# Last layer of a four-layer kernel: who rounds and subtracts the projections, and where a unit's sums are copied

## The chip, the cores and the metric

The kernel runs on one core of one Trainium2 chip, as one program on five engines: TensorE (PE, with its weight loads PEld), VectorE (DVE), ScalarE (ACT), GpSimd (POOL) and SyncE (SP, which issues DMAs here). The metric is the device time of one execution in microseconds, the median of several.

## The reference, cut to what matters

Four layers work on `x` of 2 x 2048 tokens by 256 features, each as `x = x + attn(layernorm(x)) + ffn(layernorm(x))`. The change touches only the last one, whose attention is ordinary causal attention with 16 heads of 16 features:

```python
q = split_heads(einsum('bsd,kd->bsk', x, q_proj_weight))      # 16 heads of 16
k = split_heads(...); v = split_heads(...)
scores = einsum('bhtc,bhkc->bhtk', q, k) * 16 ** -0.5
attn = softmax(where(causal, scores, -inf), axis=-1)
out = einsum('bhtk,bhkc->bhtc', attn, v)                      # then the output projection
```

Its feed-forward part is `sqrt((x @ cos(a))**2 + (x @ sin(b))**2)`, called the phase below.

## The kernel before, in words

The attention of the last layer is cut into 32 units (j, n): j = 0 to 7 is one of two sequences and a group of four heads, n = 0 to 3 is a block of 512 queries. A unit goes through two stages.

*Prep.* `pe_qk` projects q and k of 512 tokens into one PSUM bank, name `qk` (two matmuls by the weights `aWqk`). The product q.k is to be nearly exact although TensorE rounds its inputs, so each projection is split into a rounded part and a rest. ScalarE copies the bank into `hi` with rounding (`act_qk`, L2885), then VectorE subtracts `hi` from the bank and writes `lo` (`dve_qk`, L2758), which also frees the bank. SyncE then copies rows of `hi` and `lo` into the operands `QS` and `KS` with 24 DMAs (`place`, L2459), so that one matmul over 48 rows adds the three partial products. Next, `pe_prep` forms score tiles of 128 queries by up to 512 keys (rows `ps<-KS,QS`), and VectorE takes the maximum of each (L2784, or L2787 where the tile crosses the diagonal). The maxima are transposed by `pe_max` (L2592), copied to `ms` by VectorE and written into row 48 of `QS` by SyncE (`shift`, L2468).

*Main.* For each block kt of 128 keys and each pair pr of heads, `pe_main` forms two transposed score tiles (rows `ps<-QS,KS`), ScalarE takes their exponentials into `P` (L2917), GpSimd clears what lies past the diagonal in the last four kt of a unit (L2974), and TensorE multiplies by `Va` (L2636, the PV product) into a bank of its own. One pass over kt and pr is called a step here; a unit has 8n + 8. At a unit's end ScalarE copies the sums of the PV bank to `osb` (L2931), TensorE spreads each head's denominator over its rows (the sum matmul `ps<-osb,selS`), ScalarE forms its reciprocal as exp(-ln) (L2900, L2903), GpSimd multiplies (`On`, L2964), TensorE projects twice (`ps<-On,aWo`) and VectorE adds to `xT` (L2814). What follows the copy is a generator, `finish`, of which one piece is run after each step of the next unit.

The work of all stages is merged into one order by `on_clock`: each stage has a time at which it begins and a pace, and whichever is earliest goes next. Every engine walks through this same merged order and issues only its own part. Main trails prep by five clock units; a j takes ten. Every score tile, projection, sum and output product takes the next bank of one ring of seven PSUM banks (`psx`), so a matmul waits until the content of seven fills earlier has been read by ScalarE or VectorE. `beside` puts the projection for two units ahead behind the first tile of a prep unit and the transposed maxima of the unit before behind the second. GpSimd has no part in prep; its main work is written out by hand in `pool_main`.

In steady state a j has four places where a projection lies in the main work: A, when prep of n = 0 starts (main is at kt 8 of n = 2); B, prep of n = 1, just behind the boundary between main n = 2 and 3; C, prep of n = 2, in the middle of main n = 3; D, prep of n = 3, just behind the boundary between main n = 0 and 1. Two further boundaries, E (n = 1 to 2) and F (n = 3 to 0), have no projection near them.

## Time and profile before

| | us |
|---|---|
| median of 3 runs | 3794.77 (3785.83 to 3804.28) |
| the profiled execution, span from first to last instruction | 3867.5 |
| TensorE busy in it | 3519.2 (91%) |
| VectorE busy | 2473.4 (64%) |
| ScalarE busy | 1730.0 (45%) |
| GpSimd busy | 1164.8 (30%) |

Only the span is known of the profiled execution: what lies around it is not recorded apart, and with the profiler on it is longer than any of the three timed runs. A busy engine in the profile is one that has an instruction in flight. Matmul ends are modelled, so a matmul that stands in a group with a wait inside it still counts as busy. The last layer's attention takes the stretch from about 2730 us to the end.

### The profile page before, as it was taken

To read this page: it belongs to the slowest core of one execution; us is meant where nothing else is said; L and a number is where in the kernel's file an instruction comes from. 1 tells how busy PE (TensorE), PEld (TensorE's weight loads), DVE (VectorE), ACT (ScalarE), POOL (GpSimd) and SP (SyncE) were. 2 spreads that over 40 slices of the span, in tenths; PEclk is the share of its full clock that TensorE was granted. 3 is DMA by queue.
4 is the path that set the end of the run, shared out by engine and by line. 5 is a ranking of instruction groups with operands and counts; after the bars stand their busy time and mean duration, and the time that the engine had idled before them with its cause. 6 is when DMAs were issued, how large, how long until landed. Compare 5 with 4: busy or idle time off the path is not lost.

```text
span 3867.5 us, 47778 instructions
## 1 busy us (share of the span) xinstructions
PE 3519.2 (91%) x16468; PEld 2089.1 (54%) x16468; DVE 2473.4 (64%) x6381; ACT 1730.0 (45%) x3237; POOL 1164.8 (30%) x1190
## 2 busy tenths in 40 slices
PE   8899999968898988989878999998899999999998
PEld 7677777734555545545546667676543333433332
DVE  4444443455788988889865443443568788678774
ACT  2234443322234423343344544443346666666667
POOL 0322222151355555555542322223211111011111
PEclk7799999988899999999989999999889899999999
DMA  3244445321466666666750000000101011111100
GB/s 109 73 165 168 177 180 180 128 66 71 136 204 193 216 211 194 197 204 197 212 187 3 0 1 1 1 1 9 38 20 31 20 23 34 31 34 27 32 18 23
DMA packets 107154, 368.87 MB, mean 95 GB/s; under 512 B 27248, under 2 KB 41088, under 8 KB 96928
## 3 DMA queue, kind: packets, MB, share of 16 engines
q0 software_dynamic: 57664, 302.82, 24.3%
q1 hardware_dynamic: 48160, 60.90, 5.6%
q8 instruction: 131, 2.15, 0.2%
q10 hardware_dynamic: 1088, 2.10, 0.2%
q14 instruction: 111, 0.91, 0.1%
HBM read 322.59 MB, written 17.69 MB: 88 GB/s over the span
## 4 chain that ended last, share of the span: by engine, by line
PE 66%; DVE 21%; ACT 6%; issue 4%; another core or an unknown queue 2%; POOL 1%; DMA 0%; POOLq 0%; DVEq 0%; SPq 0%; ACTq 0%
PE ps L184 51%; PE ps L2636 6%; DVE pm L2784 4%; PE ps L1507 2%; DVE mi L1642 2%; DVE gathB L1719 2%; DVE ps L2787 2%; DVE hacc L1682 2%; ACT P L2917 1%; PE ps L2126 1%; DVE mx L1638 1%; PE ps L556 1%; PE ps L581 1%; PE ps L546 1%
## 5 line engine op out<-in xcount | busy, mean ns | idle before, releaser
L2917 ACT ACTIVATE P<-ps 128x512 f32<-128x512 f32 (+3 forms) x1280 | 587.3, 548 | 214.1 <-PE ps L184 212.0
L2784 DVE TENSOR_REDUCE pm<-ps 128x1 f32<-128x512 f32 x768 | 484.6, 684 | 113.3 <-PE ps L184 113.0
L1860 POOL DMA_INDIRECT gathB<-in_tab,idx x256 | 282.9, 1105 | 357.6 <-PE ps L1507 287.4
L184 PE MATMUL ps<-QS,KS 49*128 49x512 f32 (+3 forms) x1280 | 333.8, 422 | 16.2 <-DVE pm L2784 12.6
L1860 POOL DMA_INDIRECT gathA<-in_tab,idx x256 | 268.7, 1049 | 203.2 <-DVE mx L1638 125.5
L184 PE MATMUL ps<-KS,QS 48*128 48x512 f32 (+3 forms) x1280 | 309.8, 430 | 16.0 <-DVE pm L2787 5.9
L2974 POOL TENSOR_SCALAR_AFFINE_SELECT P<-P 128x256 f32<-128x256 f32 x256 | 103.8, 409 | 709.9 <-ACT P L2917 709.0
L2636 PE MATMUL ps<-P,Va 128*32 128x512 f32 (+3 forms) x2560 | 309.7, 557 | 5.8 <-POOL P L2974 2.9
L184 PEld LDWEIGHTS ps<-QS,KS 49*128 49x128 f32 x1280 | 158.2, 190 | 225.0 <-DVE pm L2784 81.8
L184 PEld LDWEIGHTS ps<-KS,QS 48*128 48x128 f32 x1280 | 145.5, 191 | 212.8 <-DVE pm L2784 66.2
L2787 DVE CUSTOM_DVE_ANT_0 ps<-ps,past 128x128 f32<-128x128 f32 (+3 forms) x512 | 240.1, 515 | 26.6 <-PE ps L184 24.6
L184 PE MATMUL ps<-f,K 128*128 128x512 f32 x1024 | 249.3, 395 | 0.0
L184 PE MATMUL ps<-WS,xn 128*128 128x512 f32 x512 | 231.4, 593 | 0.0
L184 PEld LDWEIGHTS ps<-f,K 128*128 128x128 f32 x1024 | 192.2, 188 | 46.8
L184 PE MATMUL ps<-moe,FW 128*128 128x128 f32 x1704 | 205.1, 278 | 0.3 <-ACT moe L1164 0.3
L184 PEld LDWEIGHTS ps<-moe,FW 128*128 128x128 f32 x1704 | 199.2, 195 | 0.5 <-ACT moe L1164 0.5
L1194 POOL DMA_INDIRECT FW<-in_F,fidx x71 | 71.6, 1009 | 414.0 <-PE ps L184 252.0
L1719 DVE CUSTOM_DVE_ANT_0 gathB<-hg,gathB,gte 128x512 f32<-128x512 f32 x256 | 178.3, 750 | 0.9 <-DMA gathB<-in_tab,idx 0.9
L1682 DVE SCALAR_TENSOR_TENSOR hacc<-gathA,lin,hacc 128x512 f32<-128x512 f32 x224 | 168.6, 753 | 3.9 <-DVE hacc L1682 0.5
L2387 POOL TENSOR_TENSOR f<-fa,f 128x512 fp32r<-128x512 f32 x64 | 85.5, 1336 | 258.4 <-DVE f L2259 258.4
L184 PEld LDWEIGHTS ps<-WS,xn 128*128 128x128 f32 x512 | 95.8, 191 | 111.5 <-issue 107.0
L998 DVE TENSOR_TENSOR moe<-moe,ps 128x384 f32<-128x384 f32 x71 | 39.4, 555 | 180.8 <-PE ps L184 121.5
(390 smaller groups left out, 7002.8 us busy)
## 6 DMA issues: line engine op xcount, KB each, us to landing
ys_sorted<-moe SPq DMA_DIRECT2D x71, 128.0 KB
KS<-hi SPq DMA_DIRECT2D x256, 32.0 KB, 1.9
QS<-hi SPq DMA_DIRECT2D x256, 32.0 KB, 1.9
gathA<-in_tab,idx POOLq DMA_INDIRECT x256
gathB<-in_tab,idx POOLq DMA_INDIRECT x256
KS<-lo SPq DMA_DIRECT2D x128, 32.0 KB, 1.9
QS<-lo SPq DMA_DIRECT2D x128, 32.0 KB, 2.0
out<-xT SPq DMA_DIRECT2D x8, 512.0 KB, 3.2
```

Of the source, the lines that this page charges most:

```text
L184: m = pe.matmul(out, w, x, start=start and i == 0, stop=stop and i == len(pairs) - 1, skip_group_check=True)
L1507: pe.matmul(p[:, ms], GB[:, h, 512 + m * 128:640 + m * 128], dg[h], start=False, stop=h == 7, skip_group_check=True).then_inc(*PR.pe.tick( ...
L1642: v = dve.max_index(mi[:, 4 * g + i, :], mx[:, 4 * g + i, :], p[:, i * 128:(i + 1) * 128])
L1682: dve.scalar_tensor_tensor(out=hacc[:, :], in0=GA[:, h, 256:768], scalar=lin[:, h:h + 1], in1=src, op0=ALU.mult, op1=ALU.add).then_inc(*(P ...
L1719: dve.tensor_tensor_reduce(out=GB[:, h, 0:512], in0=hg[:, :], in1=GB[:, h, 0:512], scale=gt_[:, h:h + 1], scalar=0.0, op0=ALU.mult, op1=AL ...
L1860: pool.indirect_dma_start(out=(GA, GB)[half][:, h, :], out_offset=None, in_=d[f"tab{half}"], in_offset=bass.IndirectOffsetOnAxis(ap=idx[t ...
L2387: pool.tensor_tensor(f2[m % 2][:, 1, :], fa[:, (m + 2) % 3, :], f2[m % 2][:, 0, :].bitcast(F32), ALU.subtract).then_inc(*BN.pool.tick("f2" ...
L2636: m = pe.matmul(o_[32 * hd:32 * hd + 32, off:BW], Va[:, kt, h * 17:h * 17 + 32], Pb[2 * (kt % 2) + hd // 2][:, hd % 2, off:BW], start=kt = ...
L2784: v = dve.tensor_reduce(m, p, AX.X, ALU.max)
L2787: v = dve.tensor_tensor_reduce(out=p, in0=p, in1=past[:, 512 - w:512], scale=1.0, scalar=-3.0e38, op0=ALU.add, op1=ALU.max, accum_out=m)
L2917: act.activation(P_[:, hh, off:BW], psx.tile("s2", j, n, kt, pr, hh)[:, off:BW], ACT.Exp).then_inc(*psx.emptied(MN.act, "s2", j, n, kt, pr ...
L2974: pool.affine_select(out=P_, in_=P_, compare_op=ALU.is_ge, fill=0.0, base=0, pattern=[[0, 2], [1, 128]], channel_multiplier=-1).then_inc(* ...
```

## The change

Five things are done, all in the last layer.

1. `act_qk` copies the projection twice: with rounding to `hi`, and without to `lo`. The second copy frees the bank.
2. `dve_qk` is gone. A new `pool_qk` on GpSimd subtracts `hi` from `lo` in SBUF, at the merged order's next place ("max" instead of "qk"), and `place` waits for it.
3. The copy of the PV sums to `osb` moves from the end of a unit into `finish`, behind the exponentials of the next unit's first step. ScalarE's logarithm comes two steps later than before, and its exponential of it as well.
4. TensorE's sum matmul, its two output products and VectorE's additions come one step later; GpSimd's `On` is tied to the fifth step.
5. GpSimd now walks through the merged order as well. Its memset of `Va`, which stood ahead of all its phase additions, now lies near their end.

```diff
--- before.py
+++ after.py
@@ -2449,7 +2449,7 @@
                     bs = slice(n * BW, (n + 1) * BW)
                     sp.wait_ge(*WT.pool.has(f"KS{j % 2}"))
                     sp.wait_ge(*MN.pe.has("s2", j - 2, 3, 4 * n + 3, 1, 1))
-                    sp.wait_ge(*PP.dve.has("qk", j, n))
+                    sp.wait_ge(*PP.pool.has("qk", j, n))
                     for col, to, places in ((1, KS, ((hi, 0), (hi, 16), (lo, 32))), (0, QS, ((hi, 0), (lo, 16), (hi, 32)))):
                         for pr in range(2):
                             for hh in range(2):
@@ -2639,6 +2639,7 @@
                     m.then_inc(*MN.pe.tick("pv", j, n, kt))
 
                 def finish(n):
+                    yield
                     p = psx.fill("sum", j, n)
                     pe.wait_ge(*MN.act.has("o", j, n))
                     pe.wait_all(psx.freed("sum", j, n))
@@ -2751,12 +2752,6 @@
                         dve.tensor_tensor(blk(xT, m, n), blk(xT, m, n), tmp[2 * ((2 * n + m) % 3)], ALU.add).then_inc(
                             *x_add(None, n, "phase", n, m))
                         yield
-
-            def dve_qk(dve, j, n):
-                dve.wait_ge(*placed_before(j, n))
-                dve.wait_ge(*PP.act.has("hi", j, n))
-                dve.tensor_tensor(lo[at(j, n)][:, :], psx.tile("qk", j, n), hi[at(j, n)][:, :].bitcast(F32), ALU.subtract).then_inc(
-                    *psx.emptied(PP.dve, "qk", j, n))
 
             def dve_maxima(dve, j, n, pr):
                 dve.wait_ge(*PP.dve.now())
@@ -2792,8 +2787,6 @@
                             yield
                             step += 1
                             also = beside(n, step)
-                            if also == "qk" and ahead(j, n)[0] < NJ:
-                                dve_qk(dve, *ahead(j, n))
                             if also == "max" and preceding(j, n)[0] >= 0:
                                 dve_max(dve, *preceding(j, n))
                             if also:
@@ -2806,7 +2799,7 @@
             def dve_main(dve, j, n, tail, v):
                 def finish(n):
                     b = j // 4
-                    yield from nothing(5)
+                    yield from nothing(6)
                     for m in range(2):
                         dve.wait_ge(*MN.pe.has("out", j, n, m))
                         dve.wait_ge(*x_before(4 * b + n))
@@ -2839,7 +2832,7 @@
                     yield from dve_weights(dve)
                     yield from dve_phase(dve)
 
-                dve_all(dve, everything(lambda j, n: dve_qk(dve, j, n), phase, lambda j, n: dve_prep(dve, j, n), lambda: nothing(8),
+                dve_all(dve, everything(lambda j, n: None, phase, lambda j, n: dve_prep(dve, j, n), lambda: nothing(8),
                                     lambda j, n: dve_main(dve, j, n, tail, nothing(8) if (j, n) == (3, 3) else iter(())), lambda: dve_last(dve)))
                 tail.drain()
 
@@ -2882,7 +2875,9 @@
             def act_qk(act, j, n):
                 act.wait_ge(*placed_before(j, n))
                 act.wait_ge(*PP.pe.has("qk", j, n))
-                act.activation(hi[at(j, n)][:, :], psx.tile("qk", j, n), ACT.Copy).then_inc(*PP.act.tick("hi", j, n))
+                act.activation(hi[at(j, n)][:, :], psx.tile("qk", j, n), ACT.Copy)
+                act.activation(lo[at(j, n)][:, :].bitcast(F32), psx.tile("qk", j, n), ACT.Copy).then_inc(
+                    *psx.emptied(PP.act, "qk", j, n))
 
             def act_prep(act, j, n):
                 for step in range(1, 8 * n + 9):
@@ -2896,6 +2891,9 @@
             def act_main(act, j, n, tail, v):
                 def finish(n):
                     act.wait_ge(*MN.pool.has("on", *((j, n - 1) if n else (j - 1, 3))))
+                    act.wait_ge(*MN.pe.has("pv", j, n, 4 * n + 3))
+                    act.activation(osb[:, :], po.tile("o", j, n)[:, :], ACT.Copy).then_inc(*po.emptied(MN.act, "o", j, n))
+                    yield from nothing(2)
                     act.wait_ge(*MN.pe.has("sum", j, n))
                     act.activation(inv[:, :], psx.tile("sum", j, n), ACT.Ln).then_inc(*psx.emptied(MN.act, "sum", j, n))
                     yield
@@ -2925,10 +2923,7 @@
                 yield
                 for _ in v:
                     pass
-                act.wait_ge(*MN.pool.has("on", *((j, n - 1) if n else (j - 1, 3))))
-                act.wait_ge(*MN.pe.has("pv", j, n, 4 * n + 3))
                 tail.drain()
-                act.activation(osb[:, :], po.tile("o", j, n)[:, :], ACT.Copy).then_inc(*po.emptied(MN.act, "o", j, n))
                 tail.gen = finish(n)
                 yield
 
@@ -2954,29 +2949,49 @@
                         pool.tensor_tensor(s0, s0, s1, ALU.add).then_inc(*PH.pool.tick("sum", n, m))
                         yield from nothing(3)
 
-            def pool_main(pool, j):
-
-                def divide(j, n):
-                    if j < 0:
-                        return
+            def pool_qk(pool, j, n):
+                pool.wait_ge(*PP.act.has("qk", j, n))
+                pool.tensor_tensor(lo[at(j, n)][:, :], lo[at(j, n)][:, :].bitcast(F32), hi[at(j, n)][:, :].bitcast(F32),
+                                   ALU.subtract).then_inc(*PP.pool.tick("qk", j, n))
+
+            def pool_prep(pool, j, n):
+                for step in range(1, 8 * n + 9):
+                    yield
+                    also = beside(n, step)
+                    if also == "max" and ahead(j, n)[0] < NJ:
+                        pool_qk(pool, *ahead(j, n))
+                    if also:
+                        yield
+
+            def pool_main(pool, j, n, tail, v):
+
+                def finish(n):
+                    yield from nothing(4)
                     pool.wait_ge(*MN.pe.has("out", *preceding(j, n), 1))
                     pool.wait_ge(*MN.act.has("inv", j, n))
                     pool.tensor_tensor(On[:, :], osb[:, :], inv[:, :], ALU.mult).then_inc(*MN.pool.tick("on", j, n))
-
-                for n in range(NQ):
-                    if n:
-                        divide(*preceding(j, n))
-                    for kt in range(4 * n, 4 * n + 4):
-                        off = (kt - 4 * n) * 128
-                        for pr in range(2):
+                    yield
+
+                for kt in range(4 * n + 4):
+                    off = (kt - 4 * n) * 128
+                    for pr in range(2):
+                        if kt >= 4 * n:
                             P_ = Pb[2 * (kt % 2) + pr][:, :, off:off + 128]
                             pool.wait_ge(*MN.act.has("s2", j, n, kt, pr, 1))
                             pool.affine_select(out=P_, in_=P_, compare_op=ALU.is_ge, fill=0.0, base=0, pattern=[[0, 2], [1, 128]],
                                                channel_multiplier=-1).then_inc(*MN.pool.tick("causal", j, n, kt, pr))
-                        if kt == 0:
-                            divide(*preceding(j, n))
-                if j == NJ - 1:
-                    divide(j, NQ - 1)
+                        yield
+                        tail.step()
+                        if pr == 1 and kt:
+                            if kt % 2 and kt > 2:
+                                next(v, None)
+                            yield
+                yield
+                for _ in v:
+                    pass
+                tail.drain()
+                tail.gen = finish(n)
+                yield
 
             def pool(pool):
                 pool.memset(past[:, :], 0.0).then_inc(*WT.pool.tick("past0"))
@@ -2986,13 +3001,23 @@
                 for i in range(2):
                     pool.memset(QS[i][:, :, :].bitcast(F32), 0.0)
                     pool.memset(KS[i][:, :, :].bitcast(F32), 1.0).then_inc(*WT.pool.tick(f"KS{i}"))
-                pool.wait_ge(*WT.act.total())
-                pool.wait_ge(*LN.pe.total())
-                pool.memset(Va[:, :, :], 1.0).then_inc(*PP.pool.tick("Va1"))
-                for _ in pool_phase(pool):
+                tail = Tail()
+
+                def ones():
+                    pool.wait_ge(*WT.act.total())
+                    pool.wait_ge(*LN.pe.total())
+                    pool.memset(Va[:, :, :], 1.0).then_inc(*PP.pool.tick("Va1"))
+                    yield from nothing(8)
+
+                def phase():
+                    yield from nothing(TURN)
+                    yield from pool_phase(pool)
+
+                for _ in everything(lambda j, n: pool_qk(pool, j, n), phase, lambda j, n: pool_prep(pool, j, n), ones,
+                                    lambda j, n: pool_main(pool, j, n, tail, nothing(8) if (j, n) == (3, 3) else iter(())),
+                                    lambda: nothing(1)):
                     pass
-                for j in range(NJ):
-                    pool_main(pool, j)
+                tail.drain()
 
             return {"pe": pe, "dve": dve, "act": act, "pool": pool, "sp": sp}
```

On TensorE at place D (the boundary from main unit (2, 0) to (2, 1)), in the kernel before, from the last PV product of the old unit on; `QS0,KS0` rows are main's score tiles, `KS0,QS0` rows prep's, `xn3,aWqk` is the projection:

```order
L2636 MATMUL ps3<-P3,Va 32x128 x2
L184 MATMUL ps1<-QS0,KS0 128x512 x2
L184 MATMUL ps2<-KS0,QS0 128x512 x2
L184 MATMUL ps3<-osb,selS 128x512
L184 MATMUL ps0<-QS0,KS0 128x512 x2
L184 MATMUL ps1<-xn3,aWqk 128x512 x2
L184 MATMUL ps1<-QS0,KS0 128x512
L184 MATMUL ps2<-QS0,KS0 128x512
```

The same place in the changed kernel:

```order
L2636 MATMUL ps3<-P3,Va 32x128 x2
L184 MATMUL ps1<-QS0,KS0 128x512 x2
L184 MATMUL ps2<-KS0,QS0 128x512 x2
L184 MATMUL ps3<-QS0,KS0 128x512
L184 MATMUL ps0<-QS0,KS0 128x512
L184 MATMUL ps0<-xn3,aWqk 128x512 x2
L184 MATMUL ps1<-osb,selS 128x512
L184 MATMUL ps1<-QS0,KS0 128x512
L184 MATMUL ps2<-QS0,KS0 128x512
```

The sum matmul has moved behind the score tiles of the second step and behind the projection.

On ScalarE at the same place, before, from the copy of the sums on (`P` rows are the exponentials):

```order
L2931 ACTIVATE osb<-ps3 128x512
L2917 ACTIVATE P0<-ps1 128x512 x2
L2900 ACTIVATE inv<-ps3 128x512
L2917 ACTIVATE P1<-ps0 128x512 x2
L2885 ACTIVATE hi1<-ps1 128x512
L2903 ACTIVATE inv<-inv 128x512
L2917 ACTIVATE P2<-ps1 128x512
L2917 ACTIVATE P2<-ps2 128x512
L2917 ACTIVATE P3<-ps0 128x512 x2
```

And in the changed kernel, from the first exponentials of the new unit on:

```order
L2915 ACTIVATE P0<-ps1 128x512 x2
L2895 ACTIVATE osb<-ps3 128x512
L2915 ACTIVATE P1<-ps3 128x512
L2915 ACTIVATE P1<-ps0 128x512
L2878 ACTIVATE hi1<-ps0 128x512
L2879 ACTIVATE lo1<-ps0 128x512
L2915 ACTIVATE P2<-ps1 128x512
L2915 ACTIVATE P2<-ps2 128x512
L2898 ACTIVATE inv<-ps1 128x512
L2915 ACTIVATE P3<-ps0 128x512 x2
L2901 ACTIVATE inv<-inv 128x512
```

The copy stands one pair of exponentials later, the second projection copy is new, and the two instructions on `inv` have moved from around the projection to behind it.

On GpSimd around place A in the changed kernel (the diagonal block of main unit (2, 2), between the product `On` of the unit before and of this one):

```order
L2972 TENSOR_TENSOR On<-osb,inv 128x512
L2981 AFFINE_SELECT P0<-P0 128x2x128
L2981 AFFINE_SELECT P1<-P1 128x2x128
L2981 AFFINE_SELECT P2<-P2 128x2x128
L2981 AFFINE_SELECT P3<-P3 128x2x128
L2954 TENSOR_TENSOR lo2<-lo2,hi2 128x512
L2981 AFFINE_SELECT P0<-P0 128x2x128
L2981 AFFINE_SELECT P1<-P1 128x2x128
L2981 AFFINE_SELECT P2<-P2 128x2x128
L2981 AFFINE_SELECT P3<-P3 128x2x128
L2954 TENSOR_TENSOR lo0<-lo0,hi0 128x512
```

Before, the eight selects stood in a row here. Now a subtraction lies between the fourth and the fifth.

## Rows read from the trace of the kernel before

**Rows 1.** The page's first part, busy time of the engines.

```profile
PE 3519.2 (91%) x16468; PEld 2089.1 (54%) x16468; DVE 2473.4 (64%) x6381; ACT 1730.0 (45%) x3237; POOL 1164.8 (30%) x1190
```

**Rows 2.** Windows: one j; length, busy of five engines, PEclk, DMA share, GB/s.

```profile
3141.44:3262.04 120.60, 114.89 (x686) 45.51 (x688) 98.65 (x248) 81.39 (x177) 18.04 (x36) 1.00 0.13 28
```

**Rows 3.** The chain that ended last between 2870 and 3750 us, by line.

```profile
by line: PE ps L184 43.8%; PE ps L2636 22.1%; DVE pm L2784 17.1%; DVE ps L2787 6.9%; ACT P L2917 3.7%; issue 1.7%; ACT hi L2885 1.0%; DVE pm L2787 0.9%; ACT inv L2903 0.6%; DVE lo L2758 0.6%; ACT osb L2931 0.5%; DVE mz L2764 0.4%; ACT inv L
```

**Rows 4.** Groups from 2600 us on: busy, mean ns, then idle before and releaser.

```profile
L2758 DVE TENSOR_TENSOR lo<-ps,hi 128x512 fp32r<-128x512 f32 x32 | 22.1, 692 | 72.9 <-ACT hi L2885 72.9
L2885 ACT ACTIVATE hi<-ps 128x512 fp32r<-128x512 f32 x32 | 19.1, 597 | 49.1 <-PE ps L184 49.1
L2931 ACT ACTIVATE osb<-ps 128x512 f32<-128x512 f32 x32 | 19.2, 599 | 52.2 <-PE ps L2636 52.2
L2964 POOL TENSOR_TENSOR On<-osb,inv 128x512 f32<-128x512 f32 x32 | 40.9, 1279 | 160.5 <-ACT inv L2903 134.4 <-PE ps L184 26.2
```

**Rows 5.** Waits in the same j as Rows 2: us in total, times, longest.

```profile
PEld ps L184 <- DVE pm L2784: 18.7, 33, 0.8
PEld ps L184 <- ACT P L2917: 13.9, 29, 0.8
ACT osb L2931 <- PE ps L2636: 6.3, 4, 1.9
```

**Rows 6.** Timeline at place C: start, us, instruction, count [idle before <-releaser].

```profile
3224.57 1.98 PE L184 MATMUL ps<-xn,aWqk 128*128 128x512 f32 x4
3226.65 0.60 ACT L2885 ACTIVATE hi<-ps 128x512 fp32r<-128x512 f32 x1 [2.09 <-PE ps L184]
3227.06 0.40 PE L184 MATMUL ps<-KS,QS 48*128 48x512 f32 x2
3227.15 4.03 ACT L2917 ACTIVATE P<-ps 128x512 f32<-128x512 f32 x8
3227.35 0.69 DVE L2758 TENSOR_TENSOR lo<-ps,hi 128x512 fp32r<-128x512 f32 x1 [1.86 <-ACT hi L2885]
...
3228.42 1.34 PE L184 MATMUL ps<-QS,KS 49*128 49x512 f32 x4
...
3229.26 0.18 PEld L184 LDWEIGHTS ps<-QS,KS 49*128 49x128 f32 x1 [0.31 <-ACT P L2917]
...
3231.28 2.49 DVE L2784 TENSOR_REDUCE pm<-ps 128x1 f32<-128x512 f32 x4 [0.84 <-PE ps L184]
```

**Rows 7.** Timeline at place D, same columns.

```profile
3142.45 4.01 ACT L2917 ACTIVATE P<-ps 128x512 f32<-128x512 f32 x8
3142.70 1.28 POOL L2964 TENSOR_TENSOR On<-osb,inv 128x512 f32<-128x512 f32 x1 [6.65 <-ACT inv L2903]
3142.75 1.28 DVE L2784 TENSOR_REDUCE pm<-ps 128x1 f32<-128x512 f32 x2
...
3147.74 1.09 ACT L2917 ACTIVATE P<-ps 128x512 f32<-128x512 f32 x2 [1.28 <-PE ps L184]
...
3149.30 1.07 PE L2636 MATMUL ps<-P,Va 128*32 128x512 f32 x8
```

**Rows 8.** Timeline at place A, same columns.

```profile
3192.01 0.18 PEld L184 LDWEIGHTS ps<-KS,QS 48*128 48x128 f32 x1 [0.20 <-ACT P L2917]
...
3192.03 0.41 POOL L2974 TENSOR_SCALAR_AFFINE_SELECT P<-P 128x256 f32<-128x256 f32 x1 [0.36 <-ACT P L2917]
...
3192.59 0.60 DVE L2787 CUSTOM_DVE_ANT_0 ps<-ps,past 128x384 f32<-128x384 f32 x1
```

**Rows 9.** Timeline at place B, same columns.

```profile
3207.77 1.09 ACT L2917 ACTIVATE P<-ps 128x512 f32<-128x512 f32 x2 [1.78 <-PE ps L184]
```

**Rows 10.** Timeline at the layer's start, and SyncE's issues at place A.

```profile
2776.21 3.94 POOL L2991 MEMSET Va<- 128x4608 f32 x1 [57.23 <-PE ps L184]
2790.59 0.30 PEld L184 LDWEIGHTS ps<-xn,P 128*128 128x128 f32 x2 [0.47 <-DVE pm L2787]
...
3194.84 1.55 SPq L2459 DMA_DIRECT2D KS<-hi  x2
```

## The prediction

> **What bounds the kernel now.** I began with the busy shares of the page [rows 1]. TensorE has 91% over the whole kernel and everything else far less, so work taken from another engine is worth only what TensorE waited for it. The change touches the last layer alone, so next came the windows of one j of its attention [rows 2]. At the full clock a j takes 120.60 us. TensorE shows 114.89 of these, VectorE 98.65, ScalarE 81.39, GpSimd 18.04. The reader should see that nobody is saturated except, by this count, TensorE, and that VectorE is the second. But a matmul row that contains a wait still counts as busy, so the third view was the chain of waits [rows 3]: TensorE holds about 66% of it, VectorE's maxima (L2784, L2787) 25%, the exponentials 3.7%. The steps that the change edits are small in it: `hi` 1.0%, `lo` 0.6%, `osb` 0.5%. Over the 880 us of that view these are 8.8, 5.3 and 4.4 us. That is the most that the three can give back if their place on the chain vanishes and nothing takes it.
>
> The waits of that j show the coupling [rows 5]. TensorE's weight loads wait 18.7 us for the maxima and 13.9 us for the exponentials; parts of both lie under a PV product that is still running. Score tiles for both readers share one ring of seven banks, so TensorE is held by whichever reader is late at that moment, ScalarE or VectorE. What must be asked at each projection is therefore: who frees the bank that TensorE wants next?
>
> **The change part by part.** I replay places of one j with the durations of its rows. All sums are in the time of the profiled execution, whose span of 3867.5 us is 72.7 us (1.9%) above the median; I carry the difference over to the median unscaled.
>
> *VectorE loses the subtraction.* It is 32 instructions of 692 ns, 22.1 us in all, and before them VectorE stood idle for 72.9 us waiting for `hi` [rows 4]. This looks like 95 us of relief. Most of it is not. During the projection TensorE makes no score tile for 1.98 us, so VectorE would idle there anyway. At C [rows 6] the next tiles for VectorE are started at 3227.06, take 0.40, and so are ready at about 3227.5; the subtraction occupies VectorE from 3227.35 for 0.69, to 3228.0. The real relief is some 0.5 us there. For the other places I take the length of the subtraction itself, 0.7, as the bound. Four places in each of seven j at 0.7 give 20 us, reached only if VectorE is what TensorE waits for right behind every projection.
>
> *ScalarE gains a copy.* A copy takes 597 ns [rows 4] and costs the row of instructions behind it 0.50 us, as eight exponentials in a row take 4.03 us [rows 6]. There are 32, 16 to 19 us of ScalarE's time. ScalarE has 39 us of idle time in a j [rows 2], but not at this spot: at C it has just waited 2.09 us for the projection, eight exponentials are due behind `hi`, and TensorE already needs 1.34 us for four score tiles because weight loads wait for exponentials (0.31 at 3229.26) [rows 6]. Every exponential there comes 0.50 later, so do the tiles, the PV product behind them and the next tiles for VectorE, which stands idle for them by 0.84 before 3231.28. Nobody downstream is ahead, so the shift stays: +0.5 us. At A the same holds by one bank: the second of two prep tiles waits at 3192.01 for an exponential and is read at about 3192.59 [rows 8]. Started at 3192.01 it is ready after the 0.40 of such a pair plus some 0.1, at 3192.5; with the copy that becomes 3193.0, and VectorE starts 0.4 late: +0.4 us. The relief ahead of it is lost in that wait.
>
> *The copy of the sums and what follows it.* Before, ScalarE stood idle 6.3 us per j, at four boundaries, for the last PV product [rows 5], then copied for 0.60 [rows 4], while TensorE made the next unit's first tiles in about 0.40 [rows 6]. Behind the change the wait is for those tiles, so ScalarE's idle time stays and the first exponentials come only 0.2 us earlier. At B and D, however, the logarithm used to lie ahead of the projection, in time when ScalarE had nothing to do; it now lies behind it, together with the second copy. From `hi` to the end of eight exponentials ScalarE has two instructions more, 1.0 us by 0.50 each. Against this the projection starts a little earlier, because the sum matmul stands behind it. At D the eight exponentials ended at 3146.46 and the next pair began at 3147.74, after 1.28 us of idle time [rows 7]; at B that idle time is 1.78 us [rows 9]. These gaps absorb a delay of 0.5 to 1.0 us. What is left at D is that the first output product now wants a bank of the last of these exponentials; my replay brings the PV product of 3149.30 [rows 7] to 3149.45: +0.15 us. At B I get 0. At E and F I find nothing beyond 0.3 of either sign and take 0. Bounds for a boundary: -0.2 (the earlier exponentials, fully used) to +1.0 (both instructions, nothing absorbed).
>
> *GpSimd subtracts.* The trace has no such instruction; the nearest is `On`, the same form over two SBUF tiles, 1279 ns [rows 4]. 32 of them are 41 us on an engine busy for 18 of 120 us. The rest is ready about 1.2 us later than before (0.5 for the copy, 1.28 against 0.69 for the subtraction). Who waits for it is SyncE's `place`: at A its first DMA goes out at 3194.84 [rows 10], behind the shift. The subtraction there stands behind the select that ran at 3192.03 for 0.41 [rows 8]; with the exponentials 0.5 later it runs from 3192.9 to 3194.2, still in time. The placed rows themselves are wanted two prep units later. I cost it at nothing; uncovered it would be 1.2 us per place. It also stands ahead of four selects at A, at most 1.28 us on a PV product; I take 0, since tiles and exponentials are late there by 0.4 to 0.5 anyway, and keep the 1.28 for the third rival.
>
> Whether the pass disturbs VectorE can be read: an `On` ran from 3142.70 while VectorE did two maxima in 1.28 us [rows 7], and four of them elsewhere take 2.49 [rows 6], so the maxima don't slow. The Trainium skill, "SBUF — State Buffer", section "Who interferes with whom", says that the two engines share a port pair as an exclusive lock, but that a VectorE instruction takes it only in a two-port mode or with both inputs in SBUF, and that a reduction never contends. Here each of VectorE's steady instructions reads PSUM; by that rule, the trace agrees, and nothing is added. Without its exception the rule would add up to 32 x 1.28 = 41 us.
>
> *The start.* The memset of `Va`, 3.94 us, stood ahead of the first phase addition at 2776.21 [rows 10]. It now lies between the last two of sixteen additions, where GpSimd has little to do, and ahead of the first copy to `Va`; there it could hold ScalarE by at most its 3.94 us. TensorE did not stand still for it: its visible wait in that stretch is 0.47 us at 2790.59 [rows 10]. So -0.5 us, bounds -3.94 and +3.94.
>
> **The sum.** Each place is met seven times with both stages running: 7 x (0.4 at A + 0 at B + 0.5 at C + 0.15 at D) = 7.4, less 0.5 at the start: +7 us. On the median that is 3794.8 + 7 = 3802 us, +0.2%. A difference of under 0.5% (19 us) can hardly be told from no change in measurements of this kernel.
>
> **The rivals.**
> 1. *VectorE's relief is worth its full size.* For it: the maxima are 25% of the chain and make TensorE wait more often than the exponentials do. Against it: right behind the projections the waits shown are for exponentials. If at every place TensorE is held by VectorE, the gain is 28 x 0.7 = 20 us, plus 0.2 at 31 boundaries, 26 us: 3769 to 3775.
> 2. *ScalarE becomes the bound around projections and boundaries.* Each of 28 places costs the full 0.50 (14 us), and at 14 of them (B, D) the delayed logarithm and its exponential cost up to 0.50 each more because the gaps of 1.28 and 1.78 us are not used, as TensorE needs a bank inside them: 14 us. Together +28: 3823. It decides as soon as the idle time behind B and D is gone for TensorE's purposes.
> 3. *GpSimd's order delays selects, `On`, or VectorE.* `On` follows the logarithm by fewer steps than before, and at F it has to let five selects pass and stands ahead of three. If output products wait 1.28 us at 28 places, that is +36: 3831. For it is only how tight the order is; against it is that GpSimd is busy for 15% of the time.
> 4. *No effect at all:* VectorE's relief and ScalarE's load cancel at each place: 3795. I count it with the forecast.
>
> **How the numbers follow.** Forecast with its neighbour 4: 0.58, own range 3788 to 3812. Rival 1: 0.20. Rival 2: 0.16. Rival 3: 0.06. For the range I reach half-way into rival 1 and to rival 2's value: 3777 to 3823. Rival 1 gives most of faster (0.19); part of 2 and all of 3 give slower (0.21); the rest is same (0.60).
>
> **What would show it.** In the changed profile a j at full clock should take 121 to 122 us, VectorE's busy time in it fall by 2.8 us and ScalarE's rise by about 2. Behind `hi` at A and C, weight loads should wait longer for exponentials (L2915) and less for maxima. The idle time behind the eight exponentials at B and D should shrink from 1.78 and 1.28 to about 1. `place` should still begin behind the shift. I am wrong if the waits for exponentials do not grow behind projections, if the j gets shorter than 120 us, or if output products are seen to wait for `On`.

## The result, and the profile after

The changed kernel takes 3842.14 us (median of four runs, 3839.38 to 3844.98) against 3794.47 us for the kernel before on the same chip: a ratio of 1.012, 95% interval 1.0101 to 1.014. The forecast of 3802 us and its range up to 3823 us were wrong; the change costs about 48 us by the medians.

The page of the changed kernel, busy time of the engines (answers to [rows 1]), and below it its groups of instructions from 2600 us on (answers to [rows 4]; L2954 is the subtraction, L2879 the second copy):

```profile
PE 3529.5 (92%) x16468; PEld 2087.1 (54%) x16468; DVE 2452.2 (64%) x6349; ACT 1740.2 (45%) x3269; POOL 1207.4 (31%) x1222
```

```profile
L2954 POOL TENSOR_TENSOR lo<-lo,hi 128x512 fp32r<-128x512 f32 x32 | 41.0, 1282 | 262.5 <-ACT lo L2879 262.5
L2972 POOL TENSOR_TENSOR On<-osb,inv 128x512 f32<-128x512 f32 x32 | 40.8, 1276 | 128.2 <-ACT inv L2901 65.3 <-PE ps L184 62.8
L2895 ACT ACTIVATE osb<-ps 128x512 f32<-128x512 f32 x32 | 19.3, 603 | 1.1 <-PE ps L2636 1.1
L2878 ACT ACTIVATE hi<-ps 128x512 fp32r<-128x512 f32 x32 | 19.1, 596 | 47.7 <-PE ps L184 47.7
L2879 ACT ACTIVATE lo<-ps 128x512 f32<-128x512 f32 x32 | 18.9, 591 | 0.0
```

Single instructions cost what was forecast: a copy 0.59 us, the subtraction on GpSimd 1282 ns where 1279 was taken from `On`, and ScalarE's wait for the last PV product is gone (1.1 us in all). What they do to TensorE shows in windows. Their columns are those of [rows 2]. First the kernel before: all attention from the fifth `hi` to the end, then the four stretches of the j of [rows 2] from one `hi` to the next, that is D to A, A to B, B to C and C to D. The column before the last two is the granted clock; a value between 0.50 and 1.00 is a mix of TensorE's two levels, 1.2 and 2.4 GHz.

```profile
2840.42:3867.50 1027.08, 970.38 (x5537) 387.87 (x5535) 763.15 (x1895) 662.78 (x1441) 145.66 (x289) 0.96 0.11 27
...
3141.44:3189.83 48.39, 46.42 (x273) 17.91 (x275) 39.94 (x90) 33.44 (x70) 6.65 (x12) 1.00 0.08 17
3189.83:3200.96 11.13, 10.69 (x73) 4.76 (x75) 9.22 (x34) 7.29 (x19) 2.40 (x6) 1.00 0.12 25
3200.96:3226.65 25.69, 24.76 (x139) 9.20 (x141) 19.94 (x54) 17.54 (x34) 1.27 (x1) 1.00 0.20 45
3226.65:3262.04 35.39, 33.02 (x207) 13.64 (x209) 29.56 (x70) 23.13 (x55) 7.72 (x17) 1.00 0.13 30
```

The same of the changed kernel:

```profile
2773.18:3843.20 1070.02, 1004.52 (x5537) 404.19 (x5535) 749.41 (x1867) 672.20 (x1469) 183.64 (x318) 0.92 0.11 26
...
3074.73:3124.49 49.76, 47.62 (x275) 18.29 (x275) 39.56 (x89) 34.29 (x71) 7.92 (x13) 1.00 0.08 17
3124.49:3137.66 13.17, 12.84 (x70) 6.07 (x71) 8.86 (x33) 7.17 (x19) 3.55 (x7) 0.74 0.13 29
3137.66:3164.37 26.71, 25.25 (x141) 9.30 (x141) 19.24 (x53) 18.61 (x36) 2.56 (x2) 1.00 0.21 47
3164.37:3203.27 38.90, 36.22 (x204) 14.68 (x205) 29.18 (x69) 22.92 (x54) 9.00 (x18) 0.87 0.10 21
```

Two things are to be read. First, stretches at the full clock are longer: 49.76 for 48.39 and 26.71 for 25.69 us; A to B is 11.18 where it is undisturbed. (The sum matmul, 1.0 us, moves from ahead of `hi` to behind it at B and D, so single stretches shift; only the sum over a j counts.) Second, the granted clock of the attention is 0.92 instead of 0.96. Windows of 2 us give the time at the lower level, 1.2 GHz, as 166 us instead of 86. A profile of a second run of the changed kernel (run 10) shows 131 us.

Only the last layer is compared here, since the profiled execution of before had its own 1.9% extra elsewhere. From its first `hi` to the end it takes 1138.0 us before and 1176.9 after, 38.9 more. Against the 48 us of the medians that leaves 9 which this pair of profiles does not show.

### The profile page after: what moved, and what is told of

Its sections match the earlier page's. It is cut to its first block, busy times and chain, and to the rows that moved or that the text cites. A ratio compares the mean times of both kernels' runs of the same rounds, so it can differ in the third digit from the quotient of the medians.

```text
span 3843.2 us, 47788 instructions
## 1 busy us (share of the span) xinstructions
PE 3529.5 (92%) x16468; PEld 2087.1 (54%) x16468; DVE 2452.2 (64%) x6349; ACT 1740.2 (45%) x3269; POOL 1207.4 (31%) x1222
## 4 chain that ended last, share of the span: by engine, by line
PE 67%; DVE 23%; ACT 6%; issue 3%; POOL 1%; DMA 0%; DVEq 0%; POOLq 0%; SPq 0%; ACTq 0%
PE ps L184 52%; PE ps L2636 6%; DVE pm L2779 4%; DVE mi L1642 3%; PE ps L1507 2%; DVE hacc L1682 2%; DVE gathB L1719 2%; DVE ps L2782 2%; ACT P L2915 2%; PE ps L2126 1%; DVE mx L1638 1%; PE ps L556 1%; DVE tm L1596 1%; PE ps L546 1%; PE ps L581 1%
## 5 line engine op out<-in xcount | busy, mean ns | idle before, releaser
L2636 PE MATMUL ps<-P,Va 128*32 128x512 f32 (+3 forms) x2560 | 318.0, 571 | 4.9 <-POOL P L2981 2.9
L998 DVE TENSOR_TENSOR moe<-moe,ps 128x384 f32<-128x384 f32 x71 | 39.3, 554 | 179.3 <-PE ps L184 121.6
```

Of the source, the lines that this page charges most:

```text
L2636: m = pe.matmul(o_[32 * hd:32 * hd + 32, off:BW], Va[:, kt, h * 17:h * 17 + 32], Pb[2 * (kt % 2) + hd // 2][:, hd % 2, off:BW], start=kt = ...
```

## The experiments

Four theories were kept apart: **C**, each copy of ScalarE behind a projection is paid by TensorE; **S**, the later sum matmul and chain cost at the boundaries; **R**, the two instructions of the inverse lie in ScalarE's way; **K**, the clock falls more often. Ratios are to before on the same chip in the same session. In the table, "clean j" is the sum of the four stretches at the full clock (before: 120.60), "low" the attention's time at 1.2 GHz in the profile (before: 86 us). "Split" is the change's second copy and GpSimd's subtraction, "finish" the later copy of the sums and everything behind it; all versions but the seventh keep GpSimd's new order. The numbers of "clean j" are those of a j in which the four stretches could be read at the full clock, or are put together from several j; for the changed kernel C to D is an estimate, since none of its profiles has one at the full clock. A range says that they differ from j to j; before itself has later j of up to 121.4.

| run | what | ratio, 95% interval | clean j | low |
|---|---|---|---|---|
| 1 | split alone | 1.0041, 1.0020 to 1.0061 | 122.55 | 100 |
| 2, 14 | finish alone | 1.0071, 1.0049 to 1.0093; 1.0079, 1.0047 to 1.0111 | 122.4 | 100, 111 |
| 3 | whole change, logarithm a step earlier | 1.0101, 1.0048 to 1.0155 | 122.9 | 175 |
| 4, 15 | GpSimd's order alone | 0.9978, 0.9957 to 0.9999; 0.9985, 0.9957 to 1.0013 | 120.6 | 88, 70 |
| 5 | finish, sum matmul in the third step | 1.0074, 1.0041 to 1.0107 | some 121.5 | 133 |
| 6 | finish, inverse of 8 columns | 1.0021, 0.9985 to 1.0057 | 120.9 | 79 |
| 7 | before, inverse of 8 columns | 0.9969, 0.9936 to 1.0001 | 119.9 | 55 |
| 8 | split with a third copy | 1.0111, 1.0079 to 1.0142 | 124.54 | 112 |
| 9 | whole change, spare product in step 1 | 1.0103, 1.0067 to 1.0139 | 124 | 123 |
| 10 | whole change again | 1.0116, 1.0085 to 1.0148 | 123.4 | 131 |
| 11 | finish, but sums copied at the unit's end | 1.0078, 1.0051 to 1.0106 | 122.48 | 107 |
| 12 | sums copied late, sum matmul in step 1 | 1.0304, 1.0260 to 1.0348 | none | 272 |
| 13 | finish, spare product in step 1 | 1.0022, 0.9994 to 1.0050 | 122.5 to 123.2 | 62 |
| 16 | whole change, spare products in step 1 and in the last pair of steps | 1.0075, 1.0049 to 1.0100 | 126.5 to 128 | 10 |
| 17 | order alone, spare product in the last pair of steps | 1.0022, 1.0005 to 1.0039 | 123.4 to 123.8 | 24 |
| 18 | order alone, spare product in step 2 | 1.0002, 0.9983 to 1.0021 | 121.6 to 123 | 31 |

**The halves (runs 1, 2, 4).** Run 1 leaves `finish` as before; run 2 leaves `hi` and `lo` as before; run 4 has only `pool_main` rewritten and the memset of `Va` moved.

> Only the first half of the change: ScalarE's two copies, GpSimd's subtraction in the merged order; the sums are copied at the unit's end as before. Theory S (sum's bank): the loss comes from the other half, where the sum matmul's bank is freed two steps later, by the logarithm, and the transposed maxima seven fills behind it wait for that. Then this kernel takes before plus the 0.4 to 0.5 us of the extra copy at places A and C, less up to 4 us at the start: 3790 to 3802 us. Theory C (copy): the extra copy on ScalarE is the loss; then 3825 us or more. Theory K (clock): the loss is TensorE time at half clock; then the time follows the half-clock time in the last layer, whichever half of the change is in: more than 86 us of it with a slower kernel.

> Only the second half: the sums are copied behind the next unit's first exponentials, everything of finish one step later; VectorE still subtracts. Theory S: this half carries most of the loss, 3815 to 3840 us, and TensorE's transposed maxima (L2592) wait for the logarithm at places B and D. Theory C: 3790 to 3800 us.

> The kernel before, with nothing changed but GpSimd's walk through the merged order: the memset of Va near the end of the phase additions, the output product right behind the second step. The changed kernel reached its fifth projection 4 us sooner after the first than the kernel before. If the memset's place is why, this kernel is 3 to 4 us faster than before: 3791 us. If it is not (the clock or the missing subtraction), 3794 us.

> The version with GpSimd's new order and the memset of Va between the phase additions, nothing else changed. If its 4 us at the start are all that it brings: ratio 0.998 to 1.0, and a clean j of 120.6.

The split half costs 0.41% and the finish half 0.71%; their sum, 1.12%, is the whole within the intervals. On the 3794.5 us of before, run 1's 0.41% makes 3810 us, which lies between what its two theories forecast (3802 at most, 3825 at least). The order alone costs nothing. It does not hold the subtraction nor the later `On`, so for the third rival the waits of the changed kernel decide: over the last layer TensorE's weight loads wait 4.9 us for `On` (4.2 before) and 14.8 us for selects (14.7 before). That rival is out. One j of run 1, stretch by stretch:

```profile
3066.81:3115.68 48.87, 46.54 (x273) 18.02 (x275) 39.48 (x89) 33.90 (x70) 7.87 (x13) 1.00 0.08 17
3115.68:3127.29 11.61, 11.17 (x73) 4.92 (x75) 8.79 (x33) 7.76 (x20) 3.56 (x7) 1.00 0.11 25
3127.29:3153.51 26.22, 24.86 (x139) 9.20 (x141) 19.40 (x53) 18.01 (x36) 2.51 (x2) 1.00 0.21 46
3153.51:3189.36 35.85, 33.48 (x207) 13.81 (x209) 28.95 (x69) 23.59 (x55) 8.99 (x18) 1.00 0.12 27
```

Against before that is +0.48, +0.48, +0.53 and +0.46. A stretch holds the copy of the projection at its start, so these are D, A, B and C: the copy is paid in full behind all four projections, with VectorE's 2 us of relief in the same rows (98.65 to 96.62). TensorE's weight loads wait 17.1 us for exponentials in this j (13.9 before) and 18.4 for the full-width maxima (18.7). Run 8 doubles the suspected cost:

```diff
+                act.activation(spare[:, :], psx.tile("qk", j, n), ACT.Copy)
```

> e1 with a third copy of each projection, into a spare tile that nobody reads. Theory C (each ScalarE instruction behind a projection is paid in full at every place): each of the four intervals of a j grows by another 0.50 us, 122.55 to 124.5 us, and the time by 14 us over e1's 3816.5: 3830. If ScalarE's idle time behind B and D can absorb copies, as the prediction had it, only the two intervals behind A and C grow: 3823.

Each stretch grew by another 0.5 us (49.33, 12.11, 26.71 and 36.35 at the full clock). C stands for the split alone.

**Where the finish half loses (runs 3, 5, 6, 7, 11, 12).** Its clean j is 1.8 us longer; in some of the later j it is less, since D there costs nothing. Run 3 takes one empty step away from ScalarE ahead of the logarithm, run 5 puts one ahead of the sum matmul, runs 6 and 7 compute the inverse for 8 of the 512 columns in all units but the first.

```diff
-                    yield from nothing(2)
+                    yield from nothing(1)
```

> The changed kernel with the logarithm (and its exponential) one step earlier, so that the bank of the sum matmul is freed one step earlier. Theory S: the waits of L2592 and of the tiles behind it for the logarithm go, 10 to 20 us less than the changed kernel: 3820 to 3832 us. Theory C: no difference from the changed kernel, 3842 us within 5.

> The second half of the change alone (e2), with the sum matmul one step later still, in the third step instead of the second. It then finds the copy osb done, and its bank is no longer the one that the transposed maxima take. Theory S (TensorE's waits for the copy and for the logarithm are the loss of this half): at full clock prep n=1 to prep n=2 falls from 26.7 us to 26.2 or less, a j from 122.3 to 121.5 or less, and the time by 5 to 15 us below e2's 3824.6. Theory R (the logarithm and its exponential simply lie in ScalarE's row behind the projection, whoever waits for the bank): no change of the intervals by over 0.3 us, 3824 us within 5.

```diff
-                    act.activation(inv[:, :], psx.tile("sum", j, n), ACT.Ln)
+                    act.activation(inv[:, 0:w_], psx.tile("sum", j, n)[:, 0:w_], ACT.Ln)
```

> e2 with the logarithm and its exponential over 8 of 512 columns (behind the first unit; the rest of the reciprocals is left stale, so the result is not the reference's). Theory R: each of the two takes about 0.4 us out of ScalarE's row behind a projection, so prep n=1 to n=2 falls by 0.5 to 0.8 us to about 25.9 to 26.2, and a j by 1.5 us or more, more than in the kernel before with the same cut. Theory S: at most the 0.25 us of the bank goes.

> The kernel before with the same cut as e6 (logarithm and exponential over 8 columns, result left stale). In it the logarithm lies in time when ScalarE waits for TensorE anyway, so a j shortens by the exponential at places B and D at most: 120.6 to 119.6 us or more; time 3790 to 3801 us.

An earlier logarithm gave back 0.25 us (B to C, 26.46). With a short inverse the finish half still costs 1.0 us of a j (120.9 against 119.9), so R is at most the other 0.8. Run 5, with the sum matmul later still, gives back some 0.9 us (B to C 26.04), but at a lower clock (0.937 beside 0.944 for before), and its ratio is no better; the 5 to 15 us that theory S had forecast did not come. Run 11 then puts the copy of the sums back at the unit's end and leaves only the chain late; run 12 moves the copy and leaves the sum matmul in its step (the logarithm comes one step later there, the output products and additions one, and `On` three, so it is not the copy alone).

> The kernel before, its output sums still copied at the unit's end, with only the chain behind it one to two steps later: sum product in the second step, logarithm in the third, and so on to the output products. Theory S (the loss at the boundaries, 1.84 us per j in the version with the finish half alone, comes from the sum product's and the chain's later place): same loss, a clean j of 122.0-122.6, ratio 1.006 to 1.008. Theory O (it comes from the copy's place behind the first exponentials): a clean j within 0.5 us of 120.6, ratio 0.999 to 1.002.

> The kernel before with the copy of the output sums moved behind the next unit's first two exponentials, and everything else left in its step: sum product still in the first step (TensorE then waits for the copy there), logarithm in the second. Theory O: the copy's place costs by itself, 0.4-0.6 us at each boundary and more at the sum product, a clean j of 122.4 or more, ratio 1.007 or more. Theory S: the sum product keeps its filling place but waits about 0.5-0.7 us for the copy, so a clean j of 121 to 122, and falls of the clock at E and F stay as rare as before.

Run 11, the four stretches:

```profile
2984.77:3034.56 49.79, 47.86 (x275) 18.38 (x275) 40.27 (x90) 33.78 (x70) 6.62 (x12) 1.00 0.08 17
3034.56:3045.26 10.70, 10.08 (x70) 4.76 (x71) 9.21 (x34) 6.69 (x19) 2.39 (x6) 1.00 0.11 25
3045.26:3071.98 26.72, 25.49 (x141) 9.37 (x141) 19.86 (x54) 18.12 (x35) 1.28 (x1) 1.00 0.21 46
3071.98:3107.25 35.27, 32.85 (x204) 13.60 (x205) 29.55 (x70) 22.31 (x54) 7.65 (x17) 1.00 0.12 27
```

These are run 2's stretches (49.50 to 49.8, 10.70, 26.71, 35.24) to a few hundredths. Once the sum matmul comes a step later, where ScalarE copies the sums does not matter; the later sum matmul and chain are the whole loss of this half. Run 12 shows the reverse: with the sum matmul in step 1 TensorE stands still for the late copy, and the clock falls often (272 us at 1.2 GHz). Theory O had put the ratio at 1.007 or more, theory S a j at 121 to 122 us with falls at E and F as rare as before; both reckoned with delays of 0.4 to 0.7 us at a boundary, and neither with a loss of 3%. Its timeline at E, where TensorE waits 1.55 us:

```profile
2875.51 0.60 ACT L2900 ACTIVATE osb<-ps 128x512 f32<-128x512 f32 x1
...
2876.17 0.50 PEld L184 LDWEIGHTS ps<-osb,selS 128*128 128x128 f32 x2 [1.86 <-ACT osb L2900]
2876.17 2.07 PE L184 MATMUL ps<-osb,selS 128*128 128x512 f32 x2 [1.55 <-ACT osb L2900]
```

Why the place matters can be seen in the timelines of E. Before, at full clock:

```profile
3160.77 0.49 PE L184 MATMUL ps<-QS,KS 49*128 49x512 f32 x2
...
3161.11 0.58 PE L184 MATMUL ps<-KS,QS 48*128 48x512 f32 x2
...
3161.88 1.10 PE L184 MATMUL ps<-osb,selS 128*128 128x512 f32 x2 [0.19 <-DVE pm L2784]
...
3162.91 0.57 PE L184 MATMUL ps<-QS,KS 49*128 49x512 f32 x2
```

After:

```profile
3096.12 0.18 PEld L184 LDWEIGHTS ps<-QS,KS 49*128 49x128 f32 x1 [0.41 <-DVE pm L2779]
3096.12 1.09 PE L184 MATMUL ps<-QS,KS 49*128 49x512 f32 x2
3096.67 0.60 ACT L2895 ACTIVATE osb<-ps 128x512 f32<-128x512 f32 x1
3096.72 0.18 PEld L184 LDWEIGHTS ps<-QS,KS 49*128 49x128 f32 x1 [0.41 <-DVE pm L2779]
3097.32 0.19 PEld L184 LDWEIGHTS ps<-KS,QS 48*128 48x128 f32 x2 [0.41 <-DVE pm L2779]
...
3097.74 1.12 PE L184 MATMUL ps<-osb,selS 128*128 128x512 f32 x2
```

At this boundary VectorE is behind: before, it does six maxima in a row from 3159.25 on (3.68 us) without idle time. That it is behind because main's last tiles were narrow and came fast is my reading, not shown by a run. Before, the sum matmul, 1.1 us of dense work that needs one bank, filled the time in which VectorE freed the next. Now TensorE walks through three waits of 0.41 us for VectorE, one tile at a time, and does the 1.1 us afterwards.

Two of the runs below bear this out. Run 13 puts a spare product of the same size where the sum matmul had been, four more per j. Stretch for stretch its j is only about 0.3 us longer than run 2's (from C on 35.69, 49.49, 10.89 and 26.71, for 35.54, 49.50, 10.70 and 26.71): the place takes such a product almost for nothing. Run 18 puts it into the second step, behind a sum matmul that kept the first, and there four of them make a j 0.8 to 1.6 us longer than the same j of run 4.

**The clock (runs 9, 10, 13, 14, 16 to 18).** In the versions with the finish half the clock falls at another place than before: 0.7 to 3.9 us behind the copy of the sums at E and F (10 of the 17 falls in run 10's profile; before has none at E and two at F, 6 to 7 us behind). E is the clear mark: at F, run 4, without the finish half, has three falls 0.8 to 3.0 us behind the copy too, but neither it nor runs 1 and 15 has one at E. The changed kernel at one such E, windows of 2 us from 2 us ahead of the copy:

```profile
2837.24:2839.24 2.00, 1.79 (x14) 0.84 (x6) 2.00 (x4) 0.97 (x2) 0.00 (x0) 1.00 0.24 52
2839.24:2841.24 2.00, 1.83 (x4) 0.69 (x4) 1.97 (x7) 1.58 (x4) 0.00 (x0) 0.66 0.13 30
2841.24:2843.24 2.00, 2.00 (x4) 0.49 (x6) 1.07 (x2) 0.00 (x0) 0.00 (x0) 0.50 0.00 0
2843.24:2845.24 2.00, 2.00 (x10) 0.81 (x14) 0.96 (x2) 1.39 (x3) 0.00 (x0) 0.50 0.00 0
```

The second window, in which it falls, holds four matmul records. The sum matmul behind it takes 2.06 us instead of 1.12, and ScalarE stands idle for 3.03. So a spare product was put back where the sum matmul had been, into the bank that is really filled next, with a result that nobody reads:

```diff
                 def finish(n):
+                    i_ = psx.i % len(psx.tiles)
+                    pe.wait_all([s_.has(*k_) for s_, k_ in psx.empty.get(psx.last[i_], [])])
+                    chain(pe, psx.tiles[i_][:, :], [(WQK[:, 0, 0, :], xn[:, 0, 0:BW])])
                     yield
```

> The changed kernel, with one spare product put back where the sum product stood before: in the first step of each unit TensorE multiplies projection weights by 512 columns of xn into the bank that it will really fill next (its result is overwritten; TensorE's work grows by one product per unit, no engine waits for it). Theory K2 (the changed kernel leaves TensorE a thin stretch of waiting and short tiles at the boundaries, because the dense sum product has gone from there, and its clock then falls): falls right behind the copy of the output sums at boundaries E and F vanish, the half-clock time in the attention drops from 166 us to 100 or less, the mean clock is back within 0.002 of before's, and the ratio comes down from 1.012 to 1.005-1.009, though TensorE does more. Theory W (the falls come with any delay, wherever it lies): falls unchanged, the product costs up to 0.5 us at 28 boundaries, ratio 1.012 to 1.016.

> The changed kernel itself once more, as the neighbour of the one with the spare product on the same chip. All theories: ratio 1.010 to 1.014. Theory K2 also expects the falls of the clock again at E and F, right behind the copy of the output sums, and 130 to 190 us of half clock in the attention; a theory that the first profile was an outlier expects under 100.

> The version with the finish half alone (VectorE still subtracts, ScalarE copies a projection once) with the spare product in the first step of each unit. Theory K2: no falls behind the copy of the output sums at E and F, none new at B and D since ScalarE has no second copy there, half-clock time in the attention 60 to 95 us instead of the unfilled version's, mean clock higher than the unfilled one's by 0.002 or more, and a lower time than the unfilled one by 3 us or more although TensorE multiplies more. Theory W (the falls come with any lost time, wherever it lies): they appear elsewhere, the mean clock stays, and the time is equal to or above the unfilled one's.

> The version with the finish half alone once more, as the neighbour of the one with the spare product. Both theories: ratio 1.005 to 1.009, falls of the clock at E and F right behind the copy of the output sums.

On the finish half alone the outcome is plain: TensorE does 64 more matmul records, none of the falls 0.7 to 3.9 us behind the copy of the sums at E and F is left, the mean clock of eleven runs is 0.9426 beside 0.9353 for its unfilled neighbour, run 14 (before on that chip: 0.9390), and the ratio drops from 1.0079 (1.0047 to 1.0111) to 1.0022 (0.9994 to 1.0050). The two intervals touch; set against each other directly, the eleven runs of each have means of 3871.5 and 3884.8 us, 0.3% apart with an interval of 0.1 to 0.6%. The same boundary in run 13, the two windows from the copy on:

```profile
2904.26:2906.26 2.00, 1.68 (x6) 0.73 (x6) 1.97 (x7) 1.69 (x4) 0.00 (x0) 1.00 0.15 33
2906.26:2908.26 2.00, 2.00 (x12) 0.71 (x15) 1.48 (x3) 0.64 (x2) 0.00 (x0) 1.00 0.00 0
```

On the whole change (run 9) the falls at E and F were gone as well, but four came 16 to 17 us behind C instead, in the narrow last tiles just ahead of F, where before and run 10 have one each. The mean clock rose from 0.9358 (run 10, on the same chip) to 0.9406, of 0.9451 for before, and the ratio did not move measurably: 1.0103 beside 1.0116. The theory that the thin stretch at E and F is the cause had forecast more, 1.005 to 1.009 and at most 100 us at 1.2 GHz where 123 were measured, so for the whole change one spare product is not enough. Run 16 adds a second spare product there (`if kt == 4 * n + 3 and pr == 0`).

> The changed kernel with a spare product in the first step of each unit and a second one in each unit's last pair of steps, where the tiles are 128 columns wide and TensorE waits for maxima. Theory K2 (falls follow stretches in which TensorE has short tiles and waits): the falls 16 to 17 us behind D vanish too, mean clock at or above before's, ratio 1.003 to 1.008. Theory W (falls come with lost time, wherever it lies): the falls move again and the added work is paid, ratio 1.010 to 1.016.

(What it calls 16 to 17 us behind D is the place behind C, by the places of the prediction.)

Its attention, and one j of it:

```profile
2771.32:3819.30 1047.98, 994.43 (x5665) 395.61 (x5663) 751.86 (x1867) 673.89 (x1469) 183.48 (x318) 0.99 0.11 26
...
2943.48:3069.98 126.50, 121.63 (x701) 47.28 (x700) 97.16 (x244) 83.19 (x180) 22.98 (x40) 1.00 0.12 26
```

Two falls are left, the second 1.2 us ahead of the end, of 17 in run 10's profile; the mean clock of its runs is 0.956 beside 0.947 for before. A j at full clock is 3 us longer than the unfilled one's, and yet the ratio is 1.0075 (1.0049 to 1.0100) instead of 1.012 (1.0101 to 1.0140). That speaks against the theory that falls come with lost time wherever it lies. Runs 17 and 18 put the same product into the version with the order alone:

> The version with GpSimd's new order alone (0.998 of before), with a spare product in each unit's last pair of steps. Theory K2: mean clock above before's by 0.002 or more, which is worth 5 us or more, against at most 0.3 us paid at each of 28 places (8 us): ratio 0.995 to 1.001. Theory W: clock as before, ratio 1.000 to 1.003.

> The same version with the spare product in the second step of each unit instead, behind the sum product, which keeps the first. The mirror of the finish half with a spare product in the first step. If the chain's later steps cost nothing and the later product does: the ratio of that version, 1.001 to 1.004. If the spare product hides in TensorE's wait for maxima and only the chain's later steps cost: 0.996 to 1.000, with a mean clock above before's.

The clock rose here too (0.9535 and 0.9508 beside 0.9472), but not by more than the added work costs: about 3 us of a clean j in run 17, where at most 0.3 us per place had been expected, and its ratio of 1.0022 is above the 1.001 that the clock theory allowed. The fastest version that computes everything is the order alone, 0.9978 and 0.9985 of before; only the first of the two intervals excludes 1.

## Why the prediction was wrong

**What a lower clock costs** can be read from the kernel before. C to D took 35.39 us at the full clock and 41.21 in another j:

```profile
2975.21:3016.42 41.21, 39.73 (x209) 16.03 (x211) 29.71 (x70) 23.29 (x54) 7.71 (x17) 0.79 0.11 24
```

2 x 0.21 x 41.21 = 17.3 us at half clock cost 5.8 us, a third. It is not the same everywhere: B to C of another j of before, 27.34 us at a clock of 0.938, has 3.4 us at half clock for 1.6 us, nearly half, and the two profiles of the changed kernel differ by 35 us at half clock and only by 7.5 us of attention, a fifth. The Trainium skill, "TensorE: Matmul & The Clock Gate", section "HAM oscillation — how this bites in real kernels", reckons the penalty as half of the throttled time; the trace agrees for the stretch B to C and gives less in the other two cases. Waits of TensorE that the lower clock does not lengthen would explain it; no run here tests that.

**The account.** The attention of the changed kernel is 42.9 us longer in the profile. A clean j is 123.4 us (49.76 + 11.18 + 26.71 + some 35.7, the last from run 2 with one copy more), so 7 x 2.8 = 19.6 us are longer work and waits, as an estimate by seven equal j. (166 - 86) / 3 = 27 us are the clock. The sum of 46 is 3 more than the 42.9 measured; for run 10's profile it is 19.6 + 15 = 35, and 35.4 were measured. With prices from a fifth to nearly a half for the clock, the closeness is in part luck. What is firm is that longer stretches at the full clock leave about half of the 42.9 unexplained.

Point by point:

- *The failed step is the one that is not there.* The prediction took one j at the full clock, priced the change in it and multiplied by seven. It had no term for the granted clock, though the attention before already spent 86 us at half clock. In the profile 80 us more of it came, and about half of the loss is that term: 42.9 - 19.6 = 23 us (35.4 - 19.6 = 16 in run 10's profile).
- *E and F, "nothing beyond 0.3 of either sign"; B 0 and D 0.15.* By the offsets of the PV products against before, run 2 loses 0.58, 0.36, 0.42 and 0.48 us at B, E, F and D: 1.8 per j where 0.15 was summed. (In three of the later j D is level or gains up to 0.17.) The replay followed ScalarE's instructions, which indeed gain, and moved the sum matmul behind as if its place were free. It was the filler of a wait.
- *"These gaps absorb a delay" at B and D.* Alone, the copy is paid there as at A and C, 0.53 and 0.48. Beside the finish half it is absorbed (26.71 in both, 49.76 beside 49.8). So the sentence came out right for the whole change and wrong for the mechanism.
- *0.4 at A, 0.5 at C*: measured 0.48 and 0.46 in run 1. Right.
- *VectorE's relief is worth nothing*: right. Its busy time fell by 2.0 us a j in run 1 (2.8 were forecast) and no stretch got shorter.
- *GpSimd's subtraction is free, and does not slow VectorE*: right. 1282 ns, no wait of TensorE for it is recorded, and the maxima keep 683 ns (684 before). By the port rule of the Trainium skill that the prediction names ("SBUF — State Buffer", section "Who interferes with whom"), the trace agrees. (Not each of VectorE's steady instructions reads PSUM: `mz<-pm` doesn't, but it is a reduction.) TensorE's waits for `On` and the selects exclude the third rival.
- *The start, -0.5*: the stretch from the first to the fifth `hi` went from 110.89 to 106.90 us, but the same version (runs 2 and 14) shows 109.86 and 106.91, at granted clocks of 0.91 and 0.94. Before has 0.91 as well and the changed kernel 0.94. The 4 us are mostly a fall of the clock; the memset itself is worth about 1 at most.
- The second rival (+28) comes nearest to the 19.6 of the longer stretches, in part by luck. Its first half, the copy paid at each of 28 places, is what the split alone shows (1.95 us of a j, 13.7 us in seven); in the whole change only A and C pay it. Its second half, the delayed logarithm and exponential in gaps that TensorE needs, is at most 0.8 us of a j by runs 6 and 7.
- *The signs*: a j at the full clock takes 123.4 us, not 121 to 122. ScalarE's busy time rose by 1.9 us in run 1 (about 2 forecast). The idle time behind the eight exponentials shrank to 0.48 us at B and 0.73 at D, below the forecast of about 1, and TensorE's waits for exponentials grew, as forecast.

What stays open: why the clock falls in one passage through E and not in the next, though the rows are alike (at 3096.67 of the changed kernel it stays), and so how many falls a version will have. The profile shows where they come; the time at half clock differs between two profiles of one kernel by a fifth.

## What to carry to other kernels

Before moving a long, dense matmul, look at what stands around it: if TensorE waits tile by tile for a reader there, the matmul is a filler, and moving it costs its cover and, here, the clock. A cost per round at full clock is only half of a forecast: read the time at the lower clock before, list where it begins, and ask whether the change thins TensorE's work at such places. An instruction added to the engine that frees the next bank can be paid in full, though that engine is idle for a third of the time: here it was in the split alone at all four places, and beside the finish half at two.

## What was not expected of the hardware

- Adding matmuls made kernels faster: 64 more records took 0.3% off run 14's version on the same chip (0.6% by the two ratios), and 128 more took the whole change from 1.0116 to 1.0075, each against before on its own chip; the intervals of these last two overlap, those of 1.0075 and of the first measurement, 1.012, do not.
- TensorE's clock fell to 1.2 GHz though it was never idle for long: its longest waits at E are 0.4 to 0.5 us each and it counts as busy for 1.79 of the 2 us ahead of the copy and 1.83 of the 2 us in which the clock falls. The Trainium skill, "TensorE: Matmul & The Clock Gate", section "A second HAM failure mode: psum-queue depth-cycling", describes this for another kernel, with bf16 matmuls of 512 columns: frequent short idling between groups of matmuls while PSUM banks cycle can throttle the clock. The traces agree, and runs 13 and 16 show that spare products undo it: one per boundary for the finish half alone, two per unit for the whole change. The prediction should have weighed that rule.
